# tanh of z and o written in place in the gate banks, in the recurrent stage of a decoder kernel

## The reference, cut to what matters

```python
raw = wx_t + einsum('bhd,hdgo->bhgo', h, rk) + b         # gates i, f, z, o
lfm = m + log_sigmoid(fr); mn = maximum(ir, lfm)
ig, fg = exp(ir - mn), exp(lfm - mn)
cn = fg * c + ig * tanh(zr)
nn = fg * n + ig
hn = sigmoid(og) * cn / nn
```

## Time and profile before

| what | value |
|---|---|
| median of 3 runs | 4050.81 us (4048.97 to 4053.24) |
| span of the profiled execution | 4046.7 us |
| lies around the span, against the median | 4.1 us |
| busy over the span | PE 96%, DVE 91%, ACT 80%, POOL 55% |
| the recurrent loop, 65 to 2520 us (2455 us): busy | PE 2404.94, DVE 2332.84, ACT 2232.06, POOL 1555.26 us |
| granted TensorE clock there | 1.00 of full speed |
| the rest of the kernel, from 2600 us on: granted clock | 0.99 |
| mean DMA share in the loop | 0.10 |

### The profile page before, as it was taken

The page is one execution under the profiler, slowest core; times in us unless marked ns, Lnnn a source line. Parts: engine busy times, 40 slices in busy tenths (PEclk is TensorE's granted clock), DMA queues, the critical chain, the costliest instruction groups (busy, mean ns, idle before and its releaser), DMA issues. The chain is left out here.

```text
span 4046.7 us, 170045 instructions
## 1 busy us (share of the span) xinstructions
PE 3876.7 (96%) x70778; PEld 2189.0 (54%) x70778; DVE 3681.0 (91%) x10771; ACT 3256.1 (80%) x6720; POOL 2211.6 (55%) x2425
## 2 busy tenths in 40 slices
PE   6999999999999999999999998799999999999997
PEld 3555555555555555555555554466666666666664
DVE  7999999999999999999999998788888888888886
ACT  4999999999999999999999998466666666666665
POOL 3666666666666666666666666444344443444443
PEclk9999999999999999999999999899999999999998
DMA  2000111000000000000000000000000001000000
GB/s 77 21 23 23 48 54 51 21 23 23 21 23 23 21 23 23 21 23 23 21 23 23 21 23 24 17 22 23 31 24 23 23 22 33 23 22 22 26 21 9
DMA packets 101034, 105.27 MB, mean 26 GB/s; under 512 B 17536, under 2 KB 96032, under 8 KB 99768
## 3 DMA queue, kind: packets, MB, share of 16 engines
q1 hardware_dynamic: 100264, 94.39, 8.0%
HBM read 48.68 MB, written 17.69 MB: 16 GB/s over the span
## 5 line engine op out<-in xcount | busy, mean ns | idle before, releaser
L596 POOL TENSOR_TENSOR conv_products<-normed_features,conv_taps_by_token 128x256 f32<-128x256 f32 (+1 forms) x852 | 780.4, 916 | 609.7 <-DVE convolved_features L549 358.5
L309 PE MATMUL banks<-up_centred,after_cell_features 128*32 128x336 f32 x9088 | 759.6, 452 | 0.0
L786 POOL TENSOR_TENSOR exps_of_both_halves<-scores 128x256 f32<-128x256 f32 x512 | 419.1, 842 | 619.9 <-ACT scores L1042 614.7
L285 PE MATMUL banks<-down,hidden_features 112*32 112x256 f32 x6816 | 427.5, 384 | 0.0
L365 ACT ACT_TABLE_LOAD x284 | 364.4, 1283 | 52.7 <-PE banks L265 47.8
L586 POOL TENSOR_TENSOR conv_partial_sums<-conv_products,conv_partial_sums 128x512 f32<-128x512 f32 x284 | 364.8, 1285 | 66.6 <-DVEq L485 44.4
L1042 ACT ACTIVATE scores<-scores 128x512 f32<-128x512 f32 x512 | 305.4, 626 | 116.3 <-DVE scores L1190 115.4
L309 PEld LDWEIGHTS banks<-up_centred,after_cell_features 128*32 128x32 f32 x9088 | 237.2, 109 | 270.6 <-issue 270.6
L386 ACT ACT_TABLE_LOAD x284 | 364.4, 1283 | 5.0
L1190 DVE SCALAR_TENSOR_TENSOR scores<-banks,score_top 128x512 f32<-128x512 f32 x512 | 327.7, 681 | 27.0 <-PE banks L872 26.4
L258 PE MATMUL banks<-recurrent_weights,h_features 64*32 64x256 f32 x9088 | 311.7, 383 | 1.4 <-ACT h_features L358 1.4
(11 more groups left out here) (215 smaller groups left out, 10055.6 us busy)
## 6 DMA issues: line engine op xcount, KB each, us to landing
layer_inputs<-layer_outputs SPq DMA_DIRECT2D x284, 96.0 KB, 2.0
layer_inputs<-in_x SPq DMA_DIRECT2D x285, 32.0 KB, 1.8
x_scratch<-layer_outputs SPq DMA_DIRECT2D x284, 32.0 KB, 1.8
x_tokens<-in_x SPq DMA_DIRECT2D x32, 256.0 KB, 3.1
context_features<-in_ctx SPq DMA_DIRECT2D x32, 256.0 KB, 3.8
layers_out<-x_scratch SPq DMA_DIRECT2D x32, 256.0 KB, 2.9
out<-result SPq DMA_DIRECT2D x64, 128.0 KB, 1.8
up_centred<-in_ff_up SPq DMA_DIRECT2D x1, 2688.0 KB
```

The source lines that it names most:

```text
L285: mm = nc.tensor.matmul(bank[group(l), FD, 0:D], hidt[:, i, group(l)], down[:, l, i, :], start=i == 0, stop=i == UTILES - 1, skip_group_ch ...
L309: mm = nc.tensor.matmul(bank[group(l), b, 0:UP], xmt[:, n, group(l)], up[:, l, n, at:at + UP], start=n == 0, stop=n == HALF - 1, skip_grou ...
L596: nc.gpsimd.tensor_tensor(prod[:, i:i + n], xnt[:, j % NRING].rearrange("p n t -> p (n t)")[:, None, :].broadcast_to([P, n, HALF * P]), ta ...
L786: nc.gpsimd.tensor_tensor(psum[:, i % RING, :], pr[:, i % RING, 0:S], pr[:, i % RING, S:2 * S], ALU.add).then_inc(halves_added, 1)
```

## The change: what it does, and the diff

tanh of z and tanh of o are written in place over the gates in the PSUM banks, and the SBUF tiles `zt` and `ot` go. `cell` is no longer in `FD`: it is the place of z in the gate banks. Since tanh of o writes the banks in which the cell steps now read and write, the first cell step waits for `o_done` (before: for `z_done`), and the waits for `z_done`, `td_done` and `xo_done` go, since ACT does those in order before. The statistics of `xm` move from behind `xst` to in front of the cell. Behind the edit the lines shift by 1 to 8.

```diff
-    zt, td, ot = sb("tanh_z", [P, D]), sb("tanh_half_d", [P, D]), sb("tanh_half_o", [P, D])
+    td = sb("tanh_half_d", [P, D])
...
-    cell = bank[:, FD, 0:D]
+    def gates_of(j):
+        q = 2 * (j % 2)
+        return bank[:, q:q + 2, :].rearrange("p r (n g d) -> p r n g d", n=HALF, g=GATES)
...
-                nc.scalar.activation(heads(zt[:]), gate(j, 2), ACT.Tanh).then_inc(z_done, 1)
+                nc.scalar.activation(gate(j, 2), gate(j, 2), ACT.Tanh).then_inc(z_done, 1)
...
-                nc.scalar.activation(heads(ot[:]), gate(j, 3), ACT.Tanh, scale=0.5).then_inc(o_done, 1)
+                nc.scalar.activation(gate(j, 3), gate(j, 3), ACT.Tanh, scale=0.5).then_inc(o_done, 1)
...
-                dve.wait_ge(z_done, j + 1)
-                dve.wait_ge(xo_done, j + 1)
-                nc.vector.scalar_tensor_tensor(out=cell, in0=half_r[:], scalar=-2.0, in1=zt[:], op0=ALU.mult,
+                dve.wait_ge(xm_done, j + 1)
+                nc.vector.bn_stats(stat2[:], xm[:, j % MRING]).then_inc(ln2_stat, 1)
+                dve.wait_ge(ln2_stat, j + 1)
+                nc.vector.bn_aggr(mv[:, HEADS, :], stat2[:]).then_inc(ln2_mv, 1)
+                cell = gate(j, 2)
+                dve.wait_ge(o_done, j + 1)
+                nc.vector.scalar_tensor_tensor(out=cell, in0=heads(half_r[:]), scalar=-2.0, in1=cell, op0=ALU.mult,
                                                op1=ALU.add).then_inc(cell_step, 1)
-                dve.wait_ge(td_done, j + 1)
                 dve.wait_ge(cell_step, 3 * j + 1)
-                nc.vector.scalar_tensor_tensor(out=cell, in0=td[:], scalar=1.0, in1=cell, op0=ALU.add,
+                nc.vector.scalar_tensor_tensor(out=cell, in0=heads(td[:]), scalar=1.0, in1=cell, op0=ALU.add,
                                                op1=ALU.mult).then_inc(cell_step, 1)
...
-                dve.wait_ge(o_done, j + 1)
                 dve.wait_ge(cell_step, 3 * j + 3)
                 for n in range(HALF):
-                    nc.vector.scalar_tensor_tensor(out=h[:, n * P:(n + 1) * P].rearrange("p (r d) -> p r d", r=2), in0=heads_of(ot[:], n),
+                    nc.vector.scalar_tensor_tensor(out=h[:, n * P:(n + 1) * P].rearrange("p (r d) -> p r d", r=2), in0=gates_of(j)[:, :, n, 3, :],
...
-                dve.wait_ge(xm_done, j + 1)
-                nc.vector.bn_stats(stat2[:], xm[:, j % MRING]).then_inc(ln2_stat, 1)
-                dve.wait_ge(ln2_stat, j + 1)
-                nc.vector.bn_aggr(mv[:, HEADS, :], stat2[:]).then_inc(ln2_mv, 1)
```

More of the change, by code:

```diff
@@ L187, in slstm @@
     xo_done = sem("layer_output_done")
-    cell = bank[:, FD, 0:D]
+    def gates_of(j):
+        q = 2 * (j % 2)
+        return bank[:, q:q + 2, :].rearrange("p r (n g d) -> p r n g d", n=HALF, g=GATES)
     def gate(j, g):
-        q = 2 * (j % 2)
-        return bank[:, q:q + 2, :].rearrange("p r (n g d) -> p (r n) g d", n=HALF, g=GATES)[:, :, g, :]
+        return gates_of(j).rearrange("p r n g d -> p (r n) g d")[:, :, g, :]
     def heads_of(ap, n):
@@ L529, in _ @@
                                                op0=ALU.mult, op1=ALU.mult).then_inc(hid_done, 1)
-                dve.wait_ge(z_done, j + 1)
-                dve.wait_ge(xo_done, j + 1)
-                nc.vector.scalar_tensor_tensor(out=cell, in0=half_r[:], scalar=-2.0, in1=zt[:], op0=ALU.mult,
+                dve.wait_ge(xm_done, j + 1)
[5 more added lines that the diff above has]
+                nc.vector.scalar_tensor_tensor(out=cell, in0=heads(half_r[:]), scalar=-2.0, in1=cell, op0=ALU.mult,
                                                op1=ALU.add).then_inc(cell_step, 1)
-                dve.wait_ge(td_done, j + 1)
                 dve.wait_ge(cell_step, 3 * j + 1)
-                nc.vector.scalar_tensor_tensor(out=cell, in0=td[:], scalar=1.0, in1=cell, op0=ALU.add,
+                nc.vector.scalar_tensor_tensor(out=cell, in0=heads(td[:]), scalar=1.0, in1=cell, op0=ALU.add,
                                                op1=ALU.mult).then_inc(cell_step, 1)
                 dve.wait_ge(cell_step, 3 * j + 2)
-                nc.vector.scalar_tensor_tensor(out=half_r[:], in0=cell, scalar=begun[:, j:j + 1], in1=half_r[:], op0=ALU.mult,
+                nc.vector.scalar_tensor_tensor(out=heads(half_r[:]), in0=cell, scalar=begun[:, j:j + 1], in1=heads(half_r[:]), op0=ALU.mult,
                                                op1=ALU.add).then_inc(cell_step, 1)
-                dve.wait_ge(o_done, j + 1)
                 dve.wait_ge(cell_step, 3 * j + 3)
                 for n in range(HALF):
-                    nc.vector.scalar_tensor_tensor(out=h[:, n * P:(n + 1) * P].rearrange("p (r d) -> p r d", r=2), in0=heads_of(ot[:], n),
+                    nc.vector.scalar_tensor_tensor(out=h[:, n * P:(n + 1) * P].rearrange("p (r d) -> p r d", r=2), in0=gates_of(j)[:, :, n, 3, :],
                                                    scalar=1.0, in1=heads_of(half_r[:], n), op0=ALU.add,
```

## The result

The changed kernel takes **4086.75 us** (median of 4 runs, 4084.57 to 4087.51), the kernel before on the same chip 4052.02: **34.7 us slower, ratio 1.0084, 95% interval 1.007 to 1.0099**. The prediction was 4085 (4049 to 4108), slower with a chance of .88.

A forecast was written before the change was run, and what follows sets the result against it. Bound: an 8.66 us loop of gelu, copy of xn, PE's recurrence, L383, L385, L510, L513 and L516. The held L504 adds .12 a step; 283 x .12 = 34 us on 4050.8 gives 4085 us, range 4049 to 4108.

The forecast's parts named there:

- (a): First cell step on DVE (L532): one operand from PSUM, one from SBUF, priced at .43 us instead of .79.
- (b): First cell step waits for tanh of o, so starts at 1530.87 instead of 1529.91; no cost.
- (c): Cell steps on DVE: h starts .47 us later, .44 with .03 taken off for tanh of o written to PSUM.
- (d): PE's transposes of h, held by the feed-up matmuls: the later h leaves .19 us, no cost.
- (e): DVE's statistics no longer behind xst: L558 and all behind it to L504 could start .08 us earlier; no gain.
- (f): POOL's sum, .47 us later, holds L504 (now L505) to .15 behind its end; L510 comes .14 to .15 later.
- the prediction's own second sum: Loss over the whole loop without the .03 gain for tanh of o: 283 x .15 = 42 us.
- No block: L504 isn't held by POOL, nothing in the pace-setting loop moves: time stays at 4051 us; chance .07.
- faster: Chain through h, xst, DVE's statistics, L379 and L381 sets the pace: -.11 a step, -31 us, 4020; chance .04.
- slow writes: Tanh in place in PSUM: tanh of o up to .56 later, 201 us, 4252; chance .03, smaller surcharge .08.

The follow-up runs named there:

- experiment one: Changed kernel with L505 replaced by a scalar_tensor_tensor with one operand in PSUM (writes other values into xn): 4047.63 us, ratio 0.9997 to the kernel before.
- experiment three: Changed kernel without the writes in place (z and o in SBUF, cell in FD), with the statistics move and the wait for tanh of o: 4085.9 us, ratio 1.0092.
- experiment five: Kernel before with one added 128-column sum on POOL in front of the step's first sum L586: 4074.72 us against 4049.53, ratio 1.0057.
- experiment nine: Kernel before with tanh of z written by ACT into the gate bank in PSUM, tanh of o still in SBUF: 4044.32 us against 4049.11, ratio 0.9987.
- experiment two: Kernel before with only the statistics of xm moved in front of the cell: 4047.51 us, ratio 0.9998.
- experiment four: Changed kernel with the statistics of xm put back behind xst: 4162.07 us, ratio 1.028.
- experiment six: Kernel before with ACT's copy of the transposed xn put in front of gelu: 4019.94 us, ratio 0.9926.

## Why the prediction was right

Its mechanism holds: the new wait makes the cell late, the late `xst` makes POOL late, POOL's sum then lies over L505 and holds it, and L505 delays the loop that PE waits for. Taking the hold away takes the loss away (experiment one), the wait alone makes the loss (three), and so does a late POOL sum alone (five). The size is right partly by luck, as shown below. Its steps in turn.

(a) *The first cell step* at .43: 430 ns. In experiment nine it takes 430 ns too, with tanh of z in PSUM and the step begun .50 ahead of the end of POOL's product as in the kernel before, so it was the second operand in SBUF that let POOL hold it; the prediction had left that open.

(b) *The new wait*: tanh of o to the first cell step .03 (expected .02). It is the cause of everything that follows (experiment three).

(c) *The cell*: from gelu's start to the end of `h` it was 1532.34 - 1528.78 = 3.56 and is 1553.01 - 1548.98 = 4.03: **.47 later**. The forecast took .44, with .03 off for writing to PSUM. That term is wrong: tanh of o takes 379 ns (377 before), as this line over the loop shows.

```profile
L400 ACT ACTIVATE banks<-banks x283: 379/379/380, 65.6 to 2543.2; 128x256 f32<-128x256 f32 x142
```

(d) *PE and h*: PE's transposes of h start 4.20 behind gelu's start (4.22 before), .17 behind the end of `h`, with .19 forecast. No cost.

```profile
1553.18 0.44 PE L250 MATMUL banks<-identity,h 128*128 128x128 f32 x2
```

(e) *Statistics*: counted at nothing, and nothing by themselves (experiment two). What the prediction had in its numbers and didn't say is that they make room for the wait: without their move the late `xst` costs 113 us in place of 35 (experiment four).

(f) *POOL*: L505 held to .15 behind POOL's end, as L1327 was the earlier trace rows: measured .150. So the price from a far row was exact. The rule of the Trainium skill ("SBUF — State Buffer", "Who interferes with whom") that the loser "fully blocks" would have made it about 410 ns behind POOL's end and 110 us; .15 and 34.7 us were measured. That POOL holds a DVE instruction at all, and that an instruction with one operand in PSUM isn't held, agrees with the rule (experiment one). The trace of the kernel before also has the other direction: at 593.93 us L532 and POOL's 256-column product start together, and there L532 takes .43 and the product 1.01 in place of .73.

**The size.** .12 a step was forecast, .126 in the median came; the .12 rested on the .03 that isn't there, and without it the working gives .15. The difference came from two small things that it lacked: L511, which waits for nothing now, takes 406 ns and not 421 as L510 did when it waited (.015), and POOL's sum ends 3.136 behind the start of `xst` and not 3.145 (.009). So the sum was right to .01 with an error of .03 one way and one of .024 the other. That they nearly cancel is luck; without it the forecast would have been the 42 us of the prediction's own second sum, still inside its range. All of the loss is in one place, as said: PE idles 27.8 us in 102 steps before its transposes of `xm`, .272 a step in place of .151, .12 more:

```profile
L250 PE MATMUL banks<-identity,after_cell 128*128 128x128 f32 x204 | 41.8, 286 | 27.8 <-ACT normed_features L359 27.8
```

**The rivals.** *No block* falls with L505's 671 ns, *faster* with it (and its chain shows itself in experiment four), *slow writes* with tanh of o at 379 ns and with experiment three, which loses the same without any write in place.

## What to carry to other kernels

Before moving a wait, follow what the waiting engine releases, also where that engine is off the path: here a wait of DVE made POOL late, and POOL came to lie over a DVE instruction that was on it, so that DVE was busy 38 us less and the kernel 35 us slower. The busy share didn't say what bounds the loop; the one idle gap of the busiest engine did: PE had .15 a step, the edit that closed it gave 30 us, and shortening DVE's longest step by .36 gave 5. A useless move (the statistics) can be worth 75 us next to another edit, so parts of a change have to be tried both alone and taken out.

## What the runs showed of the hardware

A `tensor_scalar` from SBUF to SBUF (128x256 fp32, two per-partition scalars, 407 ns alone) that meets a POOL instruction ended .150 behind POOL's end in the median step of the changed kernel, .150 in experiment two and .152 in experiment five, whether it had started .52, .30 or .41 ahead of that end. The first cell step with two SBUF operands ended .29 behind POOL's end in the median step, both in the kernel before (787 ns, begun .50 ahead) and in experiment six (607 ns, begun .32 ahead). With one operand in PSUM neither was held (475 ns beside POOL, 430 ns).

A tanh of 128x256 takes 377 ns from PSUM to SBUF and 379 in place in PSUM (tanh of o; tanh of z 387 and 386), but ACT's next instruction starts .30 behind its start and not .26: in ACT's rows of the changed kernel above, L395, written to PSUM, is followed by L397 after .30, and the copy L359 in front, written to SBUF, by L395 after .26. Before, with z in SBUF, L396 followed L394 after 264 ns in the median step; now it is 302. It is 302 in experiment nine too, where tanh of z goes from one PSUM bank to another, so it goes with the write to PSUM and not with writing in place.
